# Expert routing in a two-layer GNN and MoE kernel: scatter into cleared buckets, or a slot table from TensorE and a gather

## The reference, cut to what matters

```python
x = x + gnn0(layernorm(x), edges)
x = x + ffn0(layernorm(x))      # 2 of 8 experts per node, weights p1/(p1+p2), p2/(p1+p2)
x = x + gnn1(layernorm(x), edges)
x = x + ffn1(layernorm(x))      # 1 of 8 experts per node, at most C = 977 nodes per expert

# ffn0: logits = xt @ Wr + br; top-2 of the softmax; the expert's own layernorm of xt with
#       gain ln_g[e] and offset ln_b[e]; y = gelu(. @ W1[e] + b1[e]) @ W2[e] + b2[e]
# ffn1: argmax of the softmax; pos = place among the nodes of that expert; kept = pos < C
#       y = (relu(x @ w1[e] + b1[e]) @ w2[e] + b2[e]) * prob * kept; nan_to_num(y)
```

## Time and profile before

| | us |
|---|---|
| median of 3 runs | 6558.2 (6554.74 to 6558.29) |
| the profiled execution, its own time | 6560.36 |
| its span, first to last instruction | 6558.6 |
| busy on PE, DVE, POOL, ACT in it | 4742.2, 3265.5, 3639.3, 1360.8 |
| mean granted TensorE clock, as a share of 2.4 GHz | 0.872 |

### The profile page before, as it was taken

The page is one execution under the profiler, slowest core; times in us unless marked ns, Lnnn a source line. Parts: engine busy times, 40 slices in busy tenths (PEclk is TensorE's granted clock), DMA queues, the critical chain, the costliest instruction groups (busy, mean ns, idle before and its releaser), DMA issues. The chain is left out here.

```text
span 6558.6 us, 98463 instructions
## 1 busy us (share of the span) xinstructions
PE 4742.2 (72%) x19729; PEld 3561.5 (54%) x19729; DVE 3265.5 (50%) x5938; ACT 1360.8 (21%) x2977; POOL 3639.3 (55%) x3708
## 2 busy tenths in 40 slices
PE   1699999999999963099999436565656565643798
PEld 0355555555555543099999325444544444433698
DVE  6666767767777757111111334444444444454344
ACT  1333333333333311022222201010101010101122
POOL 1677777777777720512222177777777777711322
PEclk9899999999999995599999668788888887875899
DMA  6566666666666634256666455555555555542455
GB/s 219 180 172 164 163 164 162 163 165 165 163 165 166 160 94 170 87 177 183 185 185 185 134 133 141 140 139 141 139 141 139 140 139 140 138 131 103 176 199 184
DMA packets 718012, 1022.22 MB, mean 156 GB/s; under 512 B 301733, under 2 KB 531561, under 8 KB 692608
## 3 DMA queue, kind: packets, MB, share of 16 engines
q0 software_dynamic: 183456, 485.95, 28.5%
q1 hardware_dynamic: 527676, 519.31, 25.9%
q10 hardware_dynamic: 6564, 14.14, 0.6%
HBM read 868.26 MB, written 153.27 MB: 156 GB/s over the span
## 5 line engine op out<-in xcount | busy, mean ns | idle before, releaser
L774 POOL DMA_INDIRECT e_rows<-sc_table,e_eidx x3224 | 3141.4, 974 | 1007.1 <-issue 932.1
L880 PE MATMUL e_ps_o<-e_rows,e_oh 128*128 128x264 f32 x6448 | 1633.5, 398 | 53.2 <-DVE e_rows L1141 26.9
L880 PEld LDWEIGHTS e_ps_o<-e_rows,e_oh 128*128 128x128 f32 x6448 | 1230.0, 195 | 412.8 <-issue 214.0
L1141 DVE TENSOR_TENSOR e_rows<-e_rows,e_ps_w 128x1024 f32<-128x1024 f32 x806 | 969.7, 1206 | 13.2 <-issue 9.6
L1073 DVE SCALAR_TENSOR_TENSOR e_u<-e_encr,e_adst,e_ps_hd 128x512 f32<-128x512 f32 x806 | 588.1, 743 | 470.8 <-PE e_ps_X L821 391.0
L821 PE MATMUL e_ps_X<-e_u,e_hwide 128*104 128x512 f32 x1612 | 806.3, 593 | 0.0
L973 ACT COPY e_res<-e_ps_o 32x264 f32<-32x264 f32 x806 | 296.4, 368 | 2131.1 <-PE e_ps_o L886 1689.5
L851 PE MATMUL e_ps_X<-e_ident,e_alog 128*104 128x128 f32 x496 | 97.9, 361 | 828.1 <-ACT e_alog L950 828.1
L1685 PE MATMUL x_ps_h<-x_xT,x_w 128*128 128x256 f32 x2624 | 647.2, 405 | 14.6 <-DMA x_b<-in_L_ffn_b_dram 14.6
L1685 PEld LDWEIGHTS x_ps_h<-x_xT,x_w 128*128 128x128 f32 x2624 | 638.0, 337 | 19.3 <-issue 15.5
L1696 PE MATMUL x_ps_y<-x_w,x_hT 128*128 128x256 f32 x2624 | 579.9, 379 | 0.0
(11 more groups left out here) (290 smaller groups left out, 4066.7 us busy)
## 6 DMA issues: line engine op xcount, KB each, us to landing
x_w<-in_L_ffn_W_dram SPq DMA_DIRECT2D x112, 1024.0 KB
e_at<-sc_grp SPq DMA_DIRECT2D x403, 192.0 KB
x_w<-in_L_ffn_w_dram SPq DMA_DIRECT2D x60, 1024.0 KB
e_rows<-sc_table,e_eidx POOLq DMA_INDIRECT x3224
e_at<-sc_grp SPq DMA_DIRECT2D x403, 96.0 KB
sc_agg<-e_res SPq DMA_DIRECT2D x816, 33.0 KB
sc_xb<-r_zero SPq DMA_DIRECT2D x24, 1032.0 KB
x_xin<-sc_xb SPq DMA_DIRECT2D x86, 258.0 KB
```

Of the source, the lines that this page charges most:

```text
L774: pool.indirect_dma_start(rows[:, k, s, j, :], None, dr["table"][:, :], bass.IndirectOffsetOnAxis(eidx[:, k, s, j:j + 1], 0)).then_inc(s_r ...
L880: nc.tensor.matmul(ps_o[:, q, 0:ROW], oh[:, k, at_j:at_j + P], rows[:, k, s, j, :], start=(j == 0), stop=False)
L1141: nc.vector.tensor_tensor(part, part, ps_w[:, k, :, s * HEADS:(s + 1) * HEADS].unsqueeze(3).to_broadcast([P, CH, HEADS, DH]), ALU.mult).th ...
```

## The change

The routing phase is written anew and the experts take their rows in another way.

- The buckets go: no zeros over `xb`, no scatter. `xb` is now one row per node (6272 rows), written in order from the normalised rows `xn` with both weights in two extra columns, by seven plain DMAs (`keep_normed`).
- The bias add is POOL's, one 128x1792 add per chunk. The normalisation is ACT's (`Identity` with scale and offset); both layernorms of layer 0 are folded into one factor and offset per row from one set of moments, the second variance being v/(v+eps).
- The moments, factors, logits, softmax and choices are made chunk by chunk: DVE does `combine(c)`, `scores(c-1)`, `factors(c)`, `choices(c-1)`.
- After the count DVE makes two one-hot matrices per pair of tile and choice: `low`, which of 128 partitions the slot has, and `high`, which of the 120 (72 in layer 1) slot columns, times a mark that holds the tile; `lowp` is `low` times the partition. PE sums `low^T high` and `lowp^T high` over all tiles into PSUM. From the two sums DVE makes the table `who`: for each slot the row to gather, the row to write, and whether it uses the first or the second weight.
- In experts POOL gathers each block's rows of `xb` by two indirect DMAs (`fetch`), three blocks ahead, in place of SP's load; DVE reads the indices and weights out of `who` (`sources`, `take`, `targets`), in place of `rows_of`.

```diff
@@ routing, SP
-                for r0 in range(0, n_slot, 8 * P):
-                    n = min(8, (n_slot - r0) // P)
-                    sp.dma_start(xb[r0:r0 + n * P, :].rearrange("(p j) d -> p (j d)", p=P), zero[:, 0:n * XW]).then_inc(s_fill, 16)
+                def keep_normed(c):
+                    sp.wait_ge(s_wg, c + 1)
+                    sp.wait_ge(s_xn, R * (c + 1))
+                    sp.dma_start(xb[lines(c), :].rearrange("(t p) d -> p t d", p=P), xn[:, tiles(c), :]).then_inc(s_kept, 16)
@@ routing, POOL
-                pool.wait_ge(s_in, 1)
-                pool.wait_ge(s_slot, 1)
-                for t in range(NT):
-                    pool.indirect_dma_start(xb[:, :], bass.IndirectOffsetOnAxis(slot_i[:, 0, t:t + 1], 0),
-                                            xt[:, t, :], None).then_inc(s_top[t // R], 16)
...
+                for c in range(R):
+                    pool.wait_ge(s_x[c], 32 if first and c == R - 1 else 16)
+                    rows = xs[:, c * R:(c + 1) * R, :]
+                    nc.gpsimd.tensor_tensor(rows, rows, bias[:, :].unsqueeze(1).to_broadcast([P, R, D]), ALU.add).then_inc(s_bias, 1)
@@ routing, PE, after the count
+                for c in range(R):
+                    k = c % 2
+                    for j in range(R * top):
...
+                        nc.tensor.matmul(ps_m[:, 0, 0:NS], low[:, k, j, :], high[:, k, j, :], start=begin, stop=end)
+                        mm = nc.tensor.matmul(ps_m[:, 1, 0:NS], lowp[:, k, j, :], high[:, k, j, :], start=begin, stop=end)
+                    mm.then_inc(s_map, 1)
@@ routing, ACT
+                for c in range(R):
+                    roots(c)
+                    if c:
+                        powers(c - 1)
+                    act.wait_ge(s_fac, c + 1)
+                    for k in range(R):
+                        t = c * R + k
+                        nc.scalar.activation(xn[:, t, 0:D], xs[:, t, :], ACT.Identity, scale=fac[:, t:t + 1], bias=off[:, t:t + 1]).then_inc(s_xn, 1)
+                    for k in range(R):
+                        t = c * R + k
+                        act.wait_ge(s_t, t + 1)
...
+                        nc.scalar.copy(xT[:, t % XP, :, :], ps_x[:, t % XP, 0:D].rearrange("p (c n) -> p c n", c=DC)).then_inc(s_xT, 1)
@@ routing, DVE
+                def combine(c):
+                    v.wait_ge(s_ag[c % AG], 16 * (c // AG + 1))
...
+                    ts(dens, dens, 1e-10, None, ALU.max)
+                    done(nc.vector.reciprocal(dens, dens))
+                    heads = part[:, :, 0:D].rearrange("p r (h c) -> p r h c", h=HEADS)
+                    tt(heads, heads, dens.unsqueeze(3).to_broadcast([P, R, HEADS, DH]), ALU.mult)
+                    v.wait_ge(s_bias, c + 1)
+                    rows = xs[:, c * R:(c + 1) * R, :]
+                    nc.vector.tensor_tensor(rows, rows, part[:, :, 0:D], ALU.add).then_inc(s_agu, 1)
...
                 for c in range(R):
...
+                    combine(c)
+                    if c:
+                        scores(c - 1)
+                    factors(c)
+                    if c:
+                        choices(c - 1)
...
+                for c in range(R):
+                    k = c % 2
+                    if c >= 2:
+                        v.wait_ge(s_map, c - 1)
+                    lows = slot[:, 2, c * R:(c + 1) * R, :].rearrange("p t n -> p (t n)")
+                    done(nc.vector.tensor_tensor(low[:, k, :, :], iotal[:, :].unsqueeze(1).to_broadcast([P, R * top, P]),
+                                                 lows.unsqueeze(2).to_broadcast([P, R * top, P]), ALU.is_equal))
+                    nc.vector.tensor_scalar(lowp[:, k, :, :], low[:, k, :, :], iotan[:, 0:1], None, ALU.mult).then_inc(s_lowp, 1)
+                    for j in range(R * top):
+                        t, n = c * R + j // top, j % top
+                        mark = float(t + 1 + FAR * n) if first else tag[:, t:t + 1]
+                        nc.vector.tensor_scalar(high[:, k, j, :], iotab[:, :], slot[:, 1, t, n:n + 1], mark, ALU.is_equal, ALU.mult).then_inc(s_low, 1)
@@ experts, SP
-                    sp.dma_start(xin[:, k, :, :], xb[bass.ds(b * TB, TB), :].rearrange("(s p) d -> p s d", p=P)).then_inc(s_ldx[k], 16)
@@ experts, POOL
+                def fetch(k):
+                    for s in range(SUB):
+                        pool.indirect_dma_start(xin[:, k, s, :], None, xb[:, :],
+                                                bass.IndirectOffsetOnAxis(gidx[:, k, s:s + 1], 0)).then_inc(s_ldx[k], 16)
...
+                        hold(pool, s_gi, i * 2 + (k + 4), s_pq)
+                        fetch(1 - k)
+                        hold(pool, s_si, i * 2 + (k + 1), s_pq)
                         hold(pool, s_add, i * 2 + (k + 1), s_pq)
@@ experts, DVE
+                        take(i * 2 + (k + 1), 1 - k)
+                        sources(i * 2 + (k + 3), 1 - k)
...
-                        rows_of(1 - k, i * 8 + (4 * k + 4))
+                        targets(1 - k)
```

More of the change, by code:

```diff
@@ L1233, in ffn_phases @@
     n_tab = nblk_max + 8
+    NS = n_slot // P
+    FAR = 64
     xb = dr["xb"]
@@ L1417, in done, with some @@
                     v.wait_ge(s_chain, steps[0])
+                def some(ins):
+                    steps[0] += 1
+                    ins.then_inc(s_chain, 1)
                 def tt(o, a, b, op):
@@ new lines, in factors @@
+                def factors(c):
+                    cs = slice(c * R, (c + 1) * R)
+                    v.wait_ge(s_std, c + 1)
+                    if first:
+                        tt(tmp1[:, cs], std[:, 0, cs], std[:, 1, cs], ALU.mult)
+                        done(nc.vector.reciprocal(fac[:, cs], tmp1[:, cs]))
+                    else:
+                        done(nc.vector.reciprocal(fac[:, cs], std[:, 0, cs]))
+                    nc.vector.scalar_tensor_tensor(off[:, cs], mean[:, cs], -1.0, fac[:, cs], ALU.mult, ALU.mult).then_inc(s_fac, 1)
@@ L1425, in _ @@
                 nc.vector.memset(zero[:, :], 0.0).then_inc(s_zero, 1)
                 nc.vector.memset(xs[:, NT - 1, :], 0.0).then_inc(s_zero, 1)
+                some(nc.vector.memset(trow[:, 0, :], 0.0))
+                if not first:
+                    some(nc.vector.memset(xn[:, :, D + 1], 0.0))
                 done(nc.vector.memset(eps[:, :], EPS))
-                v.wait_ge(s_const, 8)
+                v.wait_ge(s_const, 11)
                 v.wait_ge(s_w, 48)
                 v.wait_ge(s_zero, 2)
+                ts(valid[:, :], iotan[:, :], float(N), None, ALU.is_lt)
@@ L1431, in _ @@
                 for c in range(R):
-                    v.wait_ge(s_x[c], 32 if first and c == R - 1 else 16)
-                    v.wait_ge(s_ag[c % 2], 16 * (c // 2 + 1))
-                    rows = xs[:, c * R:(c + 1) * R, :]
-                    sums, dens = ag[:, c % 2, :, 0:D], ag[:, c % 2, :, D:ROW]
-                    ts(dens, dens, 1e-10, None, ALU.max)
-                    done(nc.vector.reciprocal(dens, dens))
-                    for r in range(R):
-                        tt(ag[:, c % 2, r, 0:D].rearrange("p (h c) -> p h c", h=HEADS), ag[:, c % 2, r, 0:D].rearrange("p (h c) -> p h c", h=HEADS),
-                           ag[:, c % 2, r, D:ROW].unsqueeze(2).to_broadcast([P, HEADS, DH]), ALU.mult)
@@ L1484, in _ @@
-                v.wait_ge(s_l, NT)
-                tt(lg[:, :, :], ps_l[:, 0:NT, :], br[:, :].unsqueeze(1).to_broadcast([P, NT, EXP]), ALU.add)
-                v.wait_ge(s_xtn, NT * (2 if first else 1))
-                wide = lambda col: col.unsqueeze(2).to_broadcast([P, NT, EXP])
-                each = lambda row: row.unsqueeze(1).to_broadcast([P, NT, EXP])
-                def red(o, i, op):
-                    done(nc.vector.tensor_reduce(o, i, AX_X, op))
-                red(c1[:, 0, :], lg[:, :, :], ALU.max)
@@ L1599, in ffn_phases @@
             s_ldw = [sem(f"ldw{k}") for k in range(2)]
+            s_ldg = [sem(f"ldg{k}") for k in range(2)]
             s_sc = [sem(f"sc{k}") for k in range(2)]
             s_gx = [sem(f"gx{k}") for k in range(2)]
-            s_ix, s_add, s_mul, s_fl, s_pq, s_free = (sem(n) for n in ("ix", "add", "mul", "fl", "pq", "free"))
+            s_gi, s_si, s_cur, s_add, s_mul, s_fl, s_pq, s_free = (sem(n) for n in ("gi", "si", "cur", "add", "mul", "fl", "pq", "free"))
             n_sc = 16 * SUB
-            n_ldx = 16 * (3 if first else 1)
+            n_ldx = 16 * SUB
             n_ldw = 16 * 4
+            n_ldg = 16 * 2
             block = ctx.enter_context(nc.Block())
@@ L1734, in _ @@
                 v.sem_inc(s_yc, 1)
-                v.wait_ge(s_const, 3)
                 v.wait_ge(s_t, 1)
+                if first:
+                    v.wait_ge(s_ldg[0], n_ldg)
                 affine(0)
-                rows_of(0, 0)
+                take(0, 0)
+                sources(2, 0)
+                targets(0)
                 pairs = v.value_load(cnt_i[0:1, 0:1], min_val=1, max_val=(nblk_max + 1) // 2)
```

392 lines of the change are left out of this document (214 added, 178 removed).

## The result

The changed kernel takes 6312.6 us (median of four runs, 6308.3 to 6317.2) beside 6557.4 us for the kernel before; the ratio is 0.963, 95% interval 0.9618 to 0.9642. The profiled execution took 6312.2 us, with a span of 6310.5. The forecast was 6335 us, the range 6270 to 6400.

A forecast was written before the change was run, and what follows sets the result against it. Routing was taken as bound by POOL's scatter issue and serial order, experts by PE. Gains of 139.5 and 91.3 us in routing, less 5 for drains, made 225.8 off 6560.4: 6335 us, range 6270 to 6400.

The forecast's parts named there:

- First chunk: Start of each routing phase until DVE's first chunk: 11.9 us instead of 12.7, ends 11 and 13.
- Chunks and the adds: Routing's seven chunks on DVE, including 2.9 us a chunk lost to POOL's bias adds: 130.2 us in layer 0, 105.7 in layer 1.
- the price of DVE's steps: DVE's own work per routing chunk, without POOL's adds: 15.7 us in layer 0 and 12.2 in layer 1.
- The rival that the adds hold nothing: In routing, POOL's bias adds do not hold DVE: 40 us less than forecast, 6295 us; chance 0.2.
- Tail, count, slots: Routing after the chunks: DVE waits 7 and 9.3 us, count matmuls take 3.1, slots 10.8 and 10.6.
- One-hots: New one-hot steps in routing, paced by DVE with PE barely hidden: 41.6 us in layer 0, 20.6 in layer 1.
- Table and exit: End of routing: block table 3.6 and 3.3 us, 17 steps 5.4 and 4.2, exit barrier 1.2.
- Experts per block: In experts, POOL's two gathers add 2.6 us a block, yet PE keeps 15.05 us: no cost, ends 0 and +0.3.
- The rival of POOL's queue: In experts, POOL's queue becomes the pace; a round of 18.5 us would give 6618 us, slower than before; chance 0.04.
- Drain: POOL's drain at the end of experts grows by 0.04 us per added indirect DMA: 7 us or nothing, taken as 5.

## Why the prediction came out, and which steps did not

The mechanism was right for routing, and the time 22 us too high. The spans differ by 248.1 us where 225.8 were forecast. That the two are so near is in part luck: errors of up to 4 us with both signs add up to only 5 us over the two routing phases, and the experts kept their pace by 2 us a block of POOL's round, where the prediction's own figures leave 3 to 8. Step by step, layer 0, then layer 1:

- *First chunk*: 9.8 and 9.8 us, forecast 11.9. The waits for the small weights are 8.7 us.
- *Chunks and the adds*: 132.6 and 109.8 us without the tail, forecast 130.2 and 105.7. Without the 24.4 and 23.2 us that the adds cost, and 4.8 us of waits for PE in layer 1, a chunk is 15.5 and 11.7 us, forecast 15.7 and 12.2. So the price of DVE's steps held. The adds were mis-sized: 20.3 us a layer was forecast, because I took `bn_stats`, reductions and reciprocals as free cover. They are not held, but the step of two operands that comes next, 0.4 to 0.5 us after the add's start in the rows above, is; an add that begins under cover costs nearly its whole length. The rival that the adds hold nothing is refuted by the undone and the doubled add.
- In the Trainium skill, SBUF — State Buffer, section Who interferes with whom, a DVE instruction with two SBUF inputs blocks against a GpSimd instruction that reads SBUF, one like `tensor_scalar` in a two-port mode against GpSimd too, and `tensor_reduce` never does; the section leaves no partial sharing. The trace agrees: 3.88 us for the one-input `valid` and `dens`, 3.61 for `r_mean`, while beside an add the reciprocal kept its 0.50 us, the reduction its 0.21 and, in layer 1, a sum that reads its logits from PSUM its 0.22 (at 5741.39, in the add from 5740.92 to 5744.88).
- *Tail, count, slots*: 6.4, 3.1, 9.9 and 8.9, 3.1, 9.8; forecast 7, 3.1, 10.8 and 9.3, 3.1, 10.6.
- *One-hots*: 37.4 and 21.6, forecast 41.6 and 20.6. In layer 0 `lowp` took 0.69 us instead of 1.06: its 512-column row from the edges, with a 16-bit integer input, was a poor stand-in. That PE is hidden is shown by `lowp` on ScalarE.
- *Table and exit*: 9.1 and 8.0, forecast 10.2 and 8.7.
- *Experts per block*: 0, as forecast. But the reason given, much room in POOL's queue, was wrong. I wrote of 4 to 9 us for POOL's round before the 2.6 us of gathers, while with them it is 13 of 15.05 us in layer 0, because the landing of the scatter (7.2 us) stands in it ahead of the gathers. No row of the kernel before shows this landing in layer 0: POOL's next step there waits for DVE longer, 11.6 us. The rival of POOL's queue was nearer than its chance of 0.04 says: with twice the gathers POOL waits for no engine in layer 0, and three times cost some 140 us.
- *Drain*: this step failed in sign. I took 5 us more, by a count of indirect DMAs. The drains after the change (min, median, max ns; the first start is layer 0's):

```profile
L1646 POOLq DRAIN  x2: 3329/4556/5782, 3475.6 to 6303.8; - x2
```

  With the experts' next phase at 3479.80, the 3.33 us are layer 0's and the 5.78 layer 1's: 3.2 and 3.4 less than in the earlier trace rows, although 114 and 62 indirect DMAs were added. With twice the gathers it is 1.61 and 2.84, with three times 3.41 and 8.24, and the same to a few ns in every kernel of one kind. It doesn't go by the count, so the 0.04 us for each indirect DMA in the sum is refuted. What sets it is open. The two experts' phases together are 5.0 us shorter, not 5 longer: 10 of the 22 us.
- *Edges of layer 1*: 7.3 of the 22 us, seen by no step.

So the 22 us are 6.5 (routing 0), -1.1 (routing 1), 10 (experts) and 7.3 (edges), less 0.4 for the rest.

## What to carry to other kernels

Work moved to an idle engine is only free if it does not hold the busy one: a 1792-column add on POOL cost DVE 3.4 us where DVE would have needed 2.06, while ScalarE took `lowp` in 2.6 times DVE's time for nothing. When a queue holds a wait for landing between two kinds of DMA, count the landing into its round before calling the queue free. And price an overlap by running it undone, but compare that run with the kernel before, stretch by stretch, too: undone the overlap cost 132 us, and yet the scatters gave more of the gain (130 of 236 us in routing) than the chunks' stretch (96), because the old order was not as bad as one by one.

## What the runs showed of the hardware that was not expected

- An add on POOL holds the next eligible DVE step for the rest of the add, even one of 7 columns (3.61 us instead of 0.17), and is itself stretched to 5.74 us behind a wide DVE step.
- A DMA of POOL's queue that adds rows to a tile does not hold the wide steps of DVE (2.02 us beside it); some short ones take up to 0.69 us instead of 0.17.
- An accumulating scatter of 256 rows lands 7.1, 6.6 or 4.3 us after its issue on average with one, two or three times the gathers in the queue, and 3.73 or 7.30 us behind the same six gathers.
- POOL's drain repeats to some ns for one kernel and goes by no count that was tried.
